# Edge scores of a graph layer: the squared difference from ScalarE, weighed by TensorE, in every third group

## The reference, cut to what matters

```
h_r  = einsum('nf,hfd->hnd', x, W_r)                 # 8 heads x 64 = 512 features per node
diff = h_r[:, dst] - h_r[:, src]
score = s_src + s_dst + (diff . a_dif)
      + (|diff| . a_abs) + (h_r[src] * h_r[dst] . a_prd)
alpha = leaky_relu(score); softmax over the edges of one source; messages summed
```

## Time and profile before

| engine | busy us in the span | share | in the loop it does |
|---|---|---|---|
| TensorE matmul | 1305.9 | 79% | fetch 1008 x, turn 1344 x, reduce 672 records for 336 matmuls |
| VectorE | 1212.5 | 74% | subtract 336 x, times 336 x, one-hot 84 x |
| ScalarE | 980.8 | 60% | Abs 336 x (584 ns), weighting 336 x (816 ns) |
| GpSimd | 884.1 | 54% | gathers 336 x (991 ns) |

### The profile page before, as it was taken

How to read it: one execution, slowest core, us unless ns; L and a number is a source line. 1 busy time by engine, 2 the same in 40 slices (tenths; PEclk the granted TensorE clock), 3 DMA queues, 4 the chain that set the end, 5 groups by cost and what they waited for, 6 DMA issues and landing times. The chain is left out here.

```text
span 1646.3 us, 25232 instructions
## 1 busy us (share of the span) xinstructions
PE 1305.9 (79%) x6421; PEld 745.9 (45%) x6422; DVE 1212.5 (74%) x2399; ACT 980.8 (60%) x2411; POOL 884.1 (54%) x982
## 2 busy tenths in 40 slices
PE   5799948999999999995688888888880702999950
PEld 1355524555555555552344444444440301777730
DVE  8898578999999999997588888888889320222216
ACT  3455516998989898984677777777770300333310
POOL 2000036666666666662677777777767055555520
PEclk9899968999999999997799999999995955999985
DMA  6111136777777777760877766676660821333329
GB/s 209 39 58 53 58 113 172 213 205 199 208 198 207 199 207 199 208 184 2 288 194 209 200 198 201 200 201 199 199 187 2 306 103 33 115 127 127 128 96 348
DMA packets 114111, 271.34 MB, mean 165 GB/s; under 512 B 27650, under 2 KB 43766, under 8 KB 113738
## 3 DMA queue, kind: packets, MB, share of 16 engines
q0 software_dynamic: 64160, 207.60, 43.4%
q1 hardware_dynamic: 47754, 61.26, 11.1%
q10 hardware_dynamic: 2080, 1.05, 0.2%
HBM read 236.42 MB, written 33.43 MB: 164 GB/s over the span
## 5 line engine op out<-in xcount | busy, mean ns | idle before, releaser
L1096 PE MATMUL m_ps<-msg,hot 128*128 128x512 f32 x672 | 368.4, 638 | 73.8 <-ACT msg L1038 64.6
L701 POOL DMA_INDIRECT x_sb<-table_d,target x336 | 333.0, 991 | 174.6 <-PE d_ps L871 86.8
L1015 POOL DMA_INDIRECT g<-he_d,target x336 | 339.6, 1011 | 132.9 <-issue 78.7
L945 ACT ACTIVATE uv<-ab,raw_a 128x512 f32<-128x512 f32 x336 | 274.3, 816 | 11.3
L858 PE MATMUL gs_ps<-room,hot_t 128*128 x1008 | 276.4, 384 | 1.7 <-DVE hot_t L724 1.7
L1059 DVE TENSOR_TENSOR msg<-g,room 128x384 f32<-128x384 f32 x336 | 185.7, 553 | 84.9 <-DMA g<-he_d,target 81.4
L731 DVE TENSOR_TENSOR x_sb<-x_sb,gs_ps 128x512 f32<-128x512 f32 x336 | 229.2, 682 | 17.8 <-PE lin_ps L862 11.5
L940 ACT ACTIVATE ab<-d_ps 128x512 f32<-128x512 f32 x336 | 196.1, 584 | 73.4 <-PE d_ps L871 71.5
L1038 ACT ACTIVATE msg<-g,room 128x64 f32<-128x64 f32 x672 | 170.2, 339 | 111.9 <-DMA g<-he_d,target 111.7
L735 DVE TENSOR_TENSOR uv<-uv,ab 128x512 f32<-128x512 f32 x336 | 230.2, 685 | 3.3 <-ACT uv L945 2.8
L1066 DVE TENSOR_TENSOR room<-m_ps,room 128x512 f32 x336 | 229.8, 684 | 0.6
(11 more groups left out here) (284 smaller groups left out, 1711.7 us busy)
## 6 DMA issues: line engine op xcount, KB each, us to landing
x_sb<-local_d SPq DMA_DIRECT2D x84, 128.0 KB
w_sb<-in_L_ffn_W_dram SPq DMA_DIRECT2D x16, 512.0 KB, 9.2
pair_rows<-pairs_d SPq DMA_DIRECT2D x8, 1024.0 KB, 13.0
x_sb<-table_d,target POOLq DMA_INDIRECT x336
g<-he_d,target POOLq DMA_INDIRECT x336
table_d<-row POOLq DMA_DIRECT2D x20, 260.0 KB, 2.6
he_d<-he SPq DMA_DIRECT2D x20, 256.0 KB, 2.0
xn_d<-xn SPq DMA_DIRECT2D x10, 512.0 KB, 4.0
```

The source lines that it names most:

```text
L701: pool.indirect_dma_start(gd[:, r, t, :], None, table_d, bass.IndirectOffsetOnAxis(ap=k["target"][:, q + t:q + t + 1], axis=0)).then_inc(g ...
L945: act.activation(uv[:, j, c, :], ab[:, j, c, :], ACT.Identity, bias=raw[:, 0, c:c + 1], scale=raw[:, 1, c:c + 1]).then_inc(ur, 1)
L1015: pool.indirect_dma_start(g[:, r, t, :, :, :].rearrange("p c h d -> p (c h d)"), None, he_d, bass.IndirectOffsetOnAxis(ap=k["target"][:, q ...
L1096: pe.matmul(m_ps[:, i % BK, :], hot[:, r, t, :], msg[:, r, t, :, :, :].rearrange("p c h d -> p (c h d)"), start=True, stop=True).then_inc( ...
```

## The change

One line of the file changes. `SQUARED`, the set of groups that are weighed in the second way, was empty and now holds every third group: 2, 5, ..., 83, which is 28 of 84.

```
-SQUARED = frozenset(())
+SQUARED = frozenset(range(2, G, 3))
```

## The result

The changed kernel takes 1660.74 us, the median of four runs (1660.46 to 1662.59); the kernel before takes 1646.55 in the same comparison. The ratio is 1.0086 (95% interval 1.0069 to 1.0104): slower by 14.2 us, where 11.3 were forecast. The profiled execution is 1662.59 us with a span of 1660.9.

What follows compares the result with a forecast made beforehand. The prediction took TensorE as the bound in ordinary groups and VectorE in strip-step groups; 24.3 for second sets, less 11 given back and 2.0 at the loop's end, made +11.3, so 1658.0 us, range 1653 to 1663.

Steps and rivals of the forecast that it cites:

- TensorE is the bound of ordinary groups: In the loop's ordinary groups TensorE sets the pace of 5.68 us, so removing VectorE's products there buys nothing.
- Price of the second set: In squared groups of the loop, a second set of four matmuls costs TensorE 0.90 us each, 24.3 us for 27.
- The first rival: In squared groups the second set runs after the first, not behind it, 1.17 us each, giving 1665.3 us; chance 0.11.
- The rival that hides the second set: In squared groups the second set's passes hide among the first's, 0.1 us per set, giving 1636.4 us; chance 0.10.
- What comes back of the strip steps: In the loop's strip-step iterations, fewer VectorE products give back 11 of the 13.0 us; 2 us stay.
- the balance per iteration: In scan iterations, 33 and 75 are relieved by 1.80 us, 19 and 61 by 0.60 plus TensorE's 0.90; 47 by nothing.
- The third rival: In the loop the strip steps stall TensorE as before, no 11 us back, giving 1669.0 us; chance 0.05.
- d_ps: In squared groups ScalarE's longer hold of this buffer costs 0; other end 0.2 us per group, 5.6 in all.
- The loop's end: At group 83 the reduction begins 1.6 us sooner and the way to the copy shortens; forecast -2.0 us.
- The sum: For the whole kernel, 24.3 - 11 - 2.0 = +11.3 us on 1646.72, forecasting 1658.0 us.

Runs made afterwards that it cites:

- the one with the places alone: The kernel before with no squared group and the strip steps at the places of the kernel with six squared groups: 1648.19 us, ratio 1.0008.
- the repeated kernel: The changed kernel run once more, unaltered, as reference for a later group of runs, against the kernel before: 1660.15 us, ratio 1.0085.

## Why the prediction was right, and which term was off

- **TensorE is the bound of ordinary groups.** Right. 28 groups without products left the others at 5.69, and each second set made its three groups longer by 0.85.
- **Price of the second set.** Right: 0.90 forecast, 0.85 over three groups, 0.89 from start to start. 27 of them are 23.0 to 24.0 us where the sum had 24.3. The first rival, 1.17 for weights that load only after the set before, is out: the loads of L886 start at 683.46, under the passes of L883, and three groups would take 18.24. The rival that hides the second set is out by the same row. The rule of the Trainium skill (TensorE: Matmul & The Clock Gate, Part 3), that a weight load runs beside matmuls in flight only if its row group differs, is not borne out here: loads for all rows, in column strips of 32, ran beside them (683.46).
- **What comes back of the strip steps.** The source was right and the size was off. 13.0 us were there by my reading, 12.5 by the kernel with the steps behind the loop. I let all but 2 come back; measured were 8.4, and 4.1 stayed. Iteration 47 kept what I had left it (1.34 against 1.2), and the sets at 33 and 75 kept 0.4 each. What I had at next to nothing and measured 2.0 are the sets with iterations 19 and 61 (0.95 and 1.03). The step that failed was the balance per iteration: I took VectorE's demand in an iteration and set it against TensorE's. In iterations 19 and 61 TensorE has a second set to do, and I counted that time as VectorE's. But these sets cost the same where TensorE has no second set (0.93 and 1.00 with the products alone left out). VectorE spends the time waiting before the fourth subtraction, 1.42 us, and the scan stands behind that; both waits of TensorE fall between the scan and the next step (382.52). Time that passes before a step can't serve it. Moving the steps to before the wait took away all of the cost (4.1 by strips, 5.4 by medians), and so did gathering them in 18 and 19 with the scan before the wait. The third rival (nothing comes back) was right about the place and wrong about the amount.
- **d_ps.** Right: in the loop no turn waited for a Square. At the very end one does, a wait of 1.2 us in the last group.
- **The loop's end.** The size was right, 2.1 us less against 2.0 forecast: 1.6 of it the earlier start, 0.5 the shorter way to the copy. TensorE's clock stayed at 2.4 GHz, with 1.17 idle before the last sets. That less idle time is the reason isn't shown: in the kernel before with its steps behind the loop, TensorE stood idle for 3.26 us at this place and the last set still took 1.06; that end was 8.92 long and not 9.77. The five kernels here with a squared last group that were profiled where the kernel before takes 1646 us all have the full clock there; the kernel before and the one with the places alone have not. Whether the clock's part of the 2.1, some 0.85, comes from the change stays open.
- **The sum.** 23.0 (27 x 0.85) and 0.6 for the strips that took 0.3 more, less 8.4 and 2.1, make +13.1. The last copy was 13.9 later in the execution shown and 12.1 later in that of the repeated kernel (772.48), as the start of the loop moves. The medians are 14.2 and 14.1 apart. The last 1 us is not accounted for, and it is within what executions of one kernel differ by. That the forecast of 11.3 came within 3 us owes something to luck: the second sets cost 0.7 less than forecast, against 2.6 that didn't come back.

## What to carry to other kernels

When one engine bounds most of a pipeline and another bounds a few iterations of it, moving work from the second to the first costs the full price wherever it is done and pays back only in those few: six moved groups beside the peaks, with the steps put where their products were, made this kernel 0.55% faster, twenty-eight spread evenly 0.86% slower. In a list that an engine works through in order, slack has a place as well as a size; before counting on it, look whether the wait comes before or after the work that is to use it. And price the place by itself, with the work behind the loop, before changing how much of it there is.

## What the runs showed of the hardware that I had not expected

Eight fp32 matmuls of 32 columns in four column strips took 1.86 to 1.88 us in either order: two rounds of 0.44 per set of four, whether two of one strip follow each other or not.

Four kernels of the experiments ran together on another chip (number 12; the rest of the experiments ran on number 7), and there the kernel before takes 1806.64 us (1803.31 to 1812.53 in 23 runs), 10% more. In the loop the instructions last as long as elsewhere (0.68 for a subtraction, 1.06 for a reduction) and the granted clock from 300 to 740 us is 1.00 as in the kernel before, but waits without a cause in the profile appear. In this stretch of the kernel with five squared groups, TensorE's weight loads for turns waited 22.0 us for issue, in 49 places:

```profile
PEld d_ps L878 <- issue: 22.0, 49, 1.0
...
ACT ab L947 <- remote: 11.9, 9, 1.7
```

Neither row is in the list of the kernel before at 1646 us. The loop, from its first one-hot to its last, is 44 us longer than in that kernel; the larger part of the 160 comes after it, where one line of VectorE (L1073) waits 88.7 us for "remote", in 27 places. On this chip the gain of 0.55% was gone, 0.9997 (0.9984 to 1.0011), while the changed kernel's loss of 0.86% stood (1.0066 for the kernel with the matmuls in pairs, which is otherwise the changed one). Whether the chip or the time of the runs makes the difference stays open, as the kernel before was not profiled there and nothing ran on both at once.
